# Two-layer attention and expert kernel: where four indirect gathers of a group stand in the GpSimd program

## The reference

```python
xn = _layernorm(x, axis=-1)
s = _L1_attn_ref(xn, L1_attn_Mq, L1_attn_Mk, L1_attn_Mv)    # 8 heads of 64; the softmax runs over the query axis
g = _silu(_L1_ffn_ref(xn, L1_ffn_Wg, L1_ffn_bg, ...))       # one of 8 experts per row: relu(x @ W1 + b1) @ W2 + b2
x = x + s * g
```

## Time and profile before

| | |
|---|---|
| median of 3 runs | 729.48 us (728.89 to 731.94) |
| profiled execution, its own time | 725.33 us |
| its span, first to last instruction | 723.7 us, mean granted clock 0.966 |
| busy: PE, PEld, DVE, ACT, POOL | 88%, 62%, 68%, 57%, 62% of the span |
| chain that ended last | PE 41%, POOL 23%, issue 18%, DVE 8%, DMA 4%, ACT 3% |
| POOL gathers, line 1634 | 32, median 992 ns each, 579.9 to 695.3 us |
| POOL scalings, line 1658 | 128, mean 0.61 us |
| DVE maxima, line 2058 | 128, mean 1.215 us |

### The profile page before, as it was taken

One profiled execution on the slowest core, in us unless ns is written; L12 is line 12 of the kernel. 1 busy time (PEld: TensorE's weight loads), 2 busy tenths in 40 slices (PEclk: granted clock), 3 DMA queues, 4 the chain that ended last, 5 costly groups with the idle time before them and its releaser, 6 DMA issues.

```text
span 723.7 us, 19568 instructions
## 1 busy us (share of the span) xinstructions
PE 634.9 (88%) x6221; PEld 447.4 (62%) x6222; DVE 493.7 (68%) x1302; ACT 414.3 (57%) x1144; POOL 447.1 (62%) x663
## 2 busy tenths in 40 slices
PE   5889989796888897997899999996999999998993
PEld 3677767685877774774344555546999744544442
DVE  4578786567767618996489888882444567786884
ACT  2466433452444446766756776772444476777793
POOL 7575888887059899972122566663333177767682
PEclk9999999998999999997999999997999999999997
DMA  9993111154566621110010000001222111111110
GB/s 251 294 309 99 42 45 56 51 121 83 104 119 139 127 45 34 30 26 2 1 31 2 16 28 24 28 25 43 69 69 69 42 31 30 31 31 31 31 45 15
DMA packets 69466, 48.34 MB, mean 67 GB/s; under 512 B 8011, under 2 KB 63750, under 8 KB 69382
## 3 DMA queue, kind: packets, MB, share of 16 engines
q1 hardware_dynamic: 62332, 34.09, 18.2%
q0 software_dynamic: 6144, 12.63, 7.2%
q10 hardware_dynamic: 906, 0.55, 0.3%
HBM read 24.00 MB, written 23.24 MB: 65 GB/s over the span
## 4 chain that ended last, share of the span: by engine, by line
PE 41%; POOL 23%; issue 18%; DVE 8%; DMA 4%; ACT 3%; SPq 1%; DVEq 0%; POOLq 0%; ACTq 0%
PE bank L1746 6%; PE bank L1817 5%; POOL vs L1658 5%; PE bank L1826 5%; POOL pool_xy L1056 5%; PE bank L1012 4%; PE bank L1726 3%; DMA xg<-x_half 3%; PE bank L1115 2%; PE bank L1125 2%; POOL xn_all L1634 2%; POOL spacer L1051 2%; DVE nmx L2058 2%; PE bank L579 2%; PE bank L1105 1%
## 5 line engine op out<-in xcount | busy, mean ns | idle before, releaser
L1891 ACT ACTIVATE pb<-bank,nmx 128x512 f32<-128x512 f32 x256 | 173.2, 690 | 73.4 <-DVE nmx L2058 73.1
L2058 DVE TENSOR_REDUCE nmx<-bank 128x2 f32<-128x1024 f32 x128 | 155.0, 1215 | 12.6 <-PE bank L1746 11.9
L1658 POOL TENSOR_TENSOR vs<-vt_first,rz 128x256 f32<-128x256 f32 x64 | 39.2, 613 | 76.0 <-DVE rz L2034 75.4
L1227 ACT ACTIVATE turns<-bank,cols 128x128 f32<-128x128 f32 x148 | 46.2, 363 | 59.2 <-PE bank L1115 40.8
L1726 PEld LDWEIGHTS bank<-pb,vs 128*32 128x32 f32 x2048 | 54.3, 110 | 38.6 <-issue 22.9
L1726 PE MATMUL bank<-pb,vs 128*32 128x128 f32 x2048 | 69.9, 275 | 2.7 <-POOL vs L1658 2.2
L382 POOL DMA_INDIRECT x_half<-pool_xy,slot x64 | 62.1, 970 | 10.6 <-issue 10.6
L1746 PE MATMUL bank<-qk 64*128 64x512 f32 x256 | 66.2, 624 | 2.3 <-ACT pb L1891 2.2
L1746 PE MATMUL bank<-qk_first 64*128 64x512 f32 x256 | 65.5, 625 | 2.9 <-ACT pb L1891 1.7
L1658 POOL TENSOR_TENSOR vs<-vt,rz 128x256 f32<-128x256 f32 x64 | 39.1, 614 | 38.2 <-DVE rz L2034 33.8
L1691 POOL COPY xn_all<-w 128x512 f32 x39 | 23.9, 613 | 52.7 <-PE bank L1817 50.6
(11 more groups left out here) (275 smaller groups left out, 1457.9 us busy)
## 6 DMA issues: line engine op xcount, KB each, us to landing
y_half<-ys SPq DMA_DIRECT2D x74, 64.5 KB
x_half<-zero SPq DMA_DIRECT2D x2, 2368.0 KB, 16.7
xg<-x_half SPq DMA_DIRECT2D x74, 64.0 KB
x_sorted<-zero SPq DMA_DIRECT2D x1, 2496.0 KB, 18.7
xn_all<-x_sorted SPq DMA_DIRECT2D x39, 64.0 KB, 1.8
y_sorted<-xn_all SPq DMA_DIRECT2D x39, 64.0 KB, 1.6
x_all<-in_L_attn_x_dram SPq DMA_DIRECT2D x8, 256.0 KB, 6.2
w<-in_L_ffn_W_dram SPq DMA_DIRECT2D x1, 2048.0 KB, 10.3
```

The lines of the kernel that those rows point to most:

```text
L1658: pool.tensor_tensor(vs[s][:, :, :], vt[bt % 2][:, n // 2 % TT, :, :].rearrange("p j d -> p (j d)") .unsqueeze(1).broadcast_to([P, 2, D]), ...
L1891: act.activation(pb[s + ab][:, :], psum[score_banks(k) + ab], ACT.Exp, bias=nmx[:, s + ab:s + ab + 1], scale=1.0, accum_out=zz[:, s + ab:s ...
L2058: dve.tensor_reduce(nmx[:, s:s + 2], banks[:, score_banks(k):score_banks(k) + 2, :], AX.X, ALU.max, negate=True).then_inc(n_mx, 1)
```

## The change

The third and fourth gather of a group move one scaling down: they were issued at half iterations 3, 4, 5, 6 and are now issued at 3, 5, 7, 9. The gathers of groups 0 and 1, in H0, stay where they are.

```diff
                         if 0 < k < B - 1 and n % SH == 1:
                             name_rows(k + 1)
-                        if 0 < k < B - 1 and GATHER_AT <= n % SH < GATHER_AT + TT:
-                            gather_row(k + 1, n % SH - GATHER_AT)
+                        if 0 < k < B - 1 and n % SH % 2 and GATHER_AT <= n % SH < GATHER_AT + 2 * TT:
+                            gather_row(k + 1, (n % SH - GATHER_AT) // 2)
```

## The result

The changed kernel takes 723.11 us (median of 13 runs, 718.61 to 726.82) against 729.48 (13 runs, 726.21 to 736.36) in the same comparison: the ratio is 0.9911, 95% interval 0.9887 to 0.9936. That is 6.4 us or 0.9%, outside the 0.5% that counts as no change. The profiled execution's span went from 723.7 to 716.9 us. Of these 6.8 us, 0.94 lie ahead of H0 (it starts at 576.64, not 577.58), where no instruction moved; they are not the change's.

What follows compares the result with a forecast made beforehand. No engine was full; all waited for DVE, held by PE reports late under POOL's gather issues. 6.2 - 0.6 - 0.2 = 5.4 us off 729.48 gave 724.1 us, own range 721.8 to 726.5, whole range 720.8 to 730.0.

Steps and rivals of the forecast that it cites:

- What bounds it: Batches 5 and 6: no engine is full; everybody waits for DVE, whose excess waits in H1 to H5 total 8.27 us.
- (a): H1 to H5: parting the second and third gathers releases DVE earlier, gaining 0.9, 1.3, 1.0, 2.0, 1.0, sum 6.2 us.
- (c): H1, H3, H5: fourth gather's shadow over iteration 15's scores costs 0.2 us each; vs5's delay costs nothing; H6 loses 0.2.
- (b): Fourth gather, now behind vs4, which waits for DVE's reciprocal, can't hold up the report DVE waits for; no separate size.
- No change: DVE's long waits have another cause, or the third gather's shadow alone equals the pair's; 728.6 or 727.9 us; chance 0.25.
- More than forecast: All 8.27 us of DVE's excess waits in H1 to H5 goes; median 721.2 us; chance 0.12.
- Slower: Four separate gather shadows add up, costing up to 0.9 us in each of six halves; 734.9 us; chance 0.08.
- The signs: DVE's waits in H1 to H5 1.2 to 1.7 us; ACT's wait falls 5 to 6; batches 5 and 6 about 33.9.
- The rule: SBUF: only the port pair shared by DVE and GpSimd contends, so a gather can't hold PE's report; gain 0.

Runs made afterwards that it cites:

- pool_busy: Kernel before, with the gathers of groups 2 to 7 replaced by plain SP loads and POOL fillers at the same four places; 719.72 us against 729.41, ratio 0.989.
- third_by_sp: Kernel before, with only the third gather of groups 2 to 7 replaced by a plain SP load and a POOL filler; 717.29 us against 723.47, ratio 0.991.
- fourth_back: Changed kernel with the fourth gather put back ahead of vs4 (half iterations 3, 5, 6, 7); 722.7 us against 729.41 for the kernel before, ratio 0.991.
- second_by_sp: Kernel before, with only the second gather of groups 2 to 7 replaced by a plain SP load and a POOL filler; 716.69 us against 723.47, ratio 0.990.
- late: Changed kernel with the gathers of groups 2 to 7 at half iterations 3, 8, 10, 12; 720.95 us against 730.59 for the kernel before, ratio 0.987.
- pair_late: Changed kernel with gathers at half iterations 3, 5, 8, 9, a pair behind vs4; 724.59 us against 729.41 for the kernel before, ratio 0.994.
- pair_front: Changed kernel with gathers at half iterations 2, 3, 5, 7, a pair behind vs1; 722.15 us against 729.41 for the kernel before, ratio 0.992.

## Why the prediction was right

Forecast 724.1 us, 5.4 below; measured 723.11, 6.4 below by the medians and 5.8 in the stage. The sum came out as the forecast had it; that it did so closely is partly luck, since errors in both directions cancel.

- **What bounds it.** Right. DVE's waits were what everybody waited for: H1 to H5 lost 7.3 us to the issues, by pool_busy, where the sum of excess waits had said 8.27.
- **(a) The pair.** Right in size, and in place by batch. Net of the shadow that (c) charged, H1 to H5 were put at 0.7, 1.3, 0.8, 2.0, 0.8 = 5.6 us; they gave 1.17, 1.00, 0.92, 1.76, 0.87 = 5.7. That match half by half hangs on the bound: by DVE's maxima the five gains are 1.20, 0.55, 1.35, 1.33 and 1.31, also 5.7. By batch it holds with either, 1.9 and 2.6 against 2.1 and 2.8 forecast. third_by_sp shows that without the pair the gain is there. The reason was half right. "A product that ends while POOL issues an indirect DMA is reported late" does not hold of every lone issue over the turn: DVE started 0.04 us behind the turn's end in H2 of after, where I had put 0.63 us behind the issue's start (622.05, that is 0.47 behind the end). The release is 0.43 us earlier than thought. But PE's turn starts 5.28 us into the half and not 4.58 as before: the second gather held the projection's report until 0.59 us behind its end (before, 0.10), so ACT emptied the bank late, which I had not seen. Together DVE starts 5.98 us into the half, where 5.71 was forecast: H2 gained 1.0 and not 1.3 us.
- **(b) The fourth gather behind vs4.** The ordering does what was said, but it is not needed: fourth_back leaves it ahead of vs4 and is as fast. Before, the fourth gather only prolonged the arrears that the pair had made.
- **(c) The costs.** vs5 at nothing was right: it starts at 623.48 without waiting, and PE's waits for POOL's scaling are 2.0 us, 2.2 before. The fourth gather's shadow of 0.2 us in each odd half is mis-sized: in third_by_sp, where it stands elsewhere, H3 takes the same 17.00. The loss that is left, in the odd halves 0.25 us, is the second gather's: second_by_sp takes 16.75 in H3, as pool_busy does, third_by_sp 17.00. In the even ones it is 0.45, of which the third gather over the turn has 0.2 (second_by_sp 16.78 in H2, pool_busy 16.57). H6, put at 0.2 lost, gained 0.10.
- **The rivals.** No change: refuted, the waits do not come of tanh or the bank. More than forecast (all 8.27 us): the most there was is 7.3. Slower: the shadows of the four single issues do not add up to the pair's: they do hold reports, but over H1 to H5 they cost 1.55 us in place of 7.3.
- **The signs.** DVE's waits, forecast at 1.2 to 1.7, are 1.11 to 1.35; batches 5 and 6, forecast at 33.9, are 34.03; H6 keeps 13.7. ACT's wait for DVE fell by 8.9 us, not 5 to 6: a wait that is long enough to be listed is counted whole, and two fell off the list, so this sum was a poor yardstick.
- **The rule.** "SBUF — State Buffer", section "SBUF: two separate sides", in the Trainium skill, lets among the engines only the port pair shared by DVE and GpSimd contend. By it the sum was 0. pool_busy agrees in so far as POOL's fillers hold up nothing (DVE's waits of 0.89 us in H2 and H4 are those of late, where no gather stands near the turn), but PE's reports do depend on what POOL issues, and here the measurement decides.

What stays open is the mechanism inside the chip. Under a lone issue it is the report that is late and not the product: behind a held report the next ones come on time again, 0.01 us behind their recorded ends in H2 of after (619.27, 619.28). Under a pair, PE's issue of small products pauses too. Why many small products, or issues that follow each other within about 1.3 us, make it so much worse, no run shows. Nor is it shown how the 3.1 us of pair_late are lost.

## What to carry to other kernels

Don't issue two indirect DMAs of GpSimd back to back just ahead of a report of PE that everybody waits for: one instruction of 0.6 us between them took the price of a group's gathers from 1.5 us a half to 0.3. Where a pair stands decides as well: ahead (pair_front) or split otherwise (fourth_back) it cost H1 to H5 nothing more (though pair_front lost 0.9 us in H6), behind vs4 it cost 3.1 us. When a wait ends well behind the recorded end of what it waits for, look at what the other engines issued in between, not only at the engine that is named. When a small program is to give the price of an effect, see whether anything in it waits for what is delayed. When two bounds of a stage disagree, see which engine's lateness one of them measures. And when a fix works, take each of its halves away by itself: only one of the two reasons behind it was real.

## What the runs showed of the hardware

- Reports of PE are delayed by GpSimd's indirect DMA issues. With four 128x128 products per turn: not at all with one gather, up to 0.28 us with two (and only where ACT and DVE were busy), DVE's start up to 0.70 us behind three in a row. With 32 small products: up to 1.08 us (lone) and 2.2 us (pair). A filler of the same length on GpSimd does nothing.
- In the program with 32 small products a pair also makes PE's own stream pause, which costs 1.1 us a pair.
- The reports that a lone gather held are out 1.61 us after its start at the latest, before its first rows move (1.65).
- A gather that directly follows another begins 0.30 us behind it and takes 0.95 us, one behind a scaling or a filler about 0.16 us behind it; behind a scaling it takes 0.99, behind a filler 0.95.
- The undisturbed delay from a turn's recorded end to DVE's start is 0.04 us, so recorded ends of PE, though modelled, can be trusted to that in these programs.
